# Paged attention with value rows of tokens c and c+16, and scores in run order

## Reference

```python
kc = k_cache[block_table].reshape(bsz, L, HK, D)
vc = v_cache[block_table].reshape(bsz, L, HK, D)
k_all = jnp.concatenate([kc, k], axis=1)
v_all = jnp.concatenate([vc, v], axis=1)
valid_c = jnp.arange(L)[None, :] < cache_seqlens[:, None]
valid = jnp.concatenate([valid_c, jnp.ones((bsz, seqlen), dtype=bool)], axis=1)
scores = jnp.einsum('bqhd,bkhd->bhqk', q, k_all) * SCALE   # k_all, v_all repeated 4 times over heads
scores = jnp.where(valid[:, None, None, :], scores, -1e+30)
probs = jax.nn.softmax(scores, axis=-1)
o = jnp.einsum('bhqk,bkhd->bqhd', probs, v_all)
```

## Time and profile before

| | |
|---|---|
| time, median of 3 runs | 1672.35 us (1672.19 to 1674.79) |
| profiled execution, its own time | 1670.93 us |
| its span, first to last instruction | 1669.1 us |
| mean granted TensorE clock | 0.996 |
| busy over the span: PE, PEld, DVE, ACT, POOL | 1611.0, 1407.2, 1113.8, 943.9, 303.9 us |
| `cached_attention`: first score product to last value product | 857.2 to 1455.6 us |
| moved by DMA over the span | 290.69 MB, mean 174 GB/s |

### The profile page before, as it was taken

One profiled execution on the slowest core, in us unless ns is written; L12 is line 12 of the kernel. 1 busy time (PEld: TensorE's weight loads), 2 busy tenths in 40 slices (PEclk: granted clock), 3 DMA queues, 4 the chain that ended last, 5 costly groups with the idle time before them and its releaser, 6 DMA issues. The chain is left out here.

```text
span 1669.1 us, 33975 instructions
## 1 busy us (share of the span) xinstructions
PE 1611.0 (97%) x10728; PEld 1407.2 (84%) x10728; DVE 1113.8 (67%) x2941; ACT 943.9 (57%) x2392; POOL 303.9 (18%) x306
## 2 busy tenths in 40 slices
PE   2899999999999999999979999999999999999998
PEld 2787888888888788888868999999999999977777
DVE  8404543454446657777767898898989889864443
ACT  3224223232322256667667999999999999822221
POOL 1000000000000146556531112111211211022210
PEclk9999999999999999999989999999999999999999
DMA  6621222201210333434567999999999999595401
GB/s 232 210 91 50 69 70 69 69 18 51 69 63 27 140 109 119 135 109 134 157 221 255 315 308 287 319 306 304 297 315 306 289 316 309 185 315 148 120 9 51
DMA packets 230095, 290.69 MB, mean 174 GB/s; under 512 B 17658, under 2 KB 181914, under 8 KB 221850
## 3 DMA queue, kind: packets, MB, share of 16 engines
q1 hardware_dynamic: 220826, 222.90, 42.5%
q0 software_dynamic: 9216, 67.11, 11.5%
HBM read 237.44 MB, written 50.41 MB: 172 GB/s over the span
## 5 line engine op out<-in xcount | busy, mean ns | idle before, releaser
L1602 PE MATMUL p_val<-probs_t,vals 128*128 128x128 f32 x2048 | 271.1, 276 | 1.7 <-DMA vals<-in_v_pages,rows_now 1.7
L1602 PEld LDWEIGHTS p_val<-probs_t,vals 128*128 128x128 f32 x2048 | 251.8, 193 | 2.0 <-DMA vals<-in_v_pages,rows_now 2.0
L1512 DVE CUSTOM_DVE_ANT_0 probs<-p_score,mask 128x544 f32<-128x544 f32 x256 | 184.4, 721 | 50.2 <-issue 40.6
L1417 ACT ACTIVATE probs<-probs,low 128x544 f32<-128x544 f32 x256 | 190.1, 743 | 0.7 <-DVE low L1512 0.7
L1581 PE MATMUL p_turn<-cst,probs 128*128 128x128 f32 x1024 | 166.3, 285 | 0.1
L1501 DVE TENSOR_TENSOR wo_lo<-keys,wo_hi 128x544 fp32r<-128x544 f32 x224 | 161.8, 722 | 0.7 <-ACT wo_hi L1412 0.7
L1425 ACT ACTIVATE probs_t<-p_turn 128x512 f32<-128x512 f32 x256 | 149.2, 583 | 19.9 <-PE p_turn L1581 19.7
L457 PE MATMUL p_tile<-w_hi,y_hi 128*128 128x512 f32 x384 | 156.7, 408 | 2.4 <-PEq L470 2.4
L1071 POOL TENSOR_TENSOR w_lo<-w_raw,w_hi 128x512 fp32r<-128x512 f32 x44 | 57.8, 1319 | 548.2 <-DVE w_hi L1109 531.1
L1412 ACT ACTIVATE wo_hi<-keys 128x544 fp32r<-128x544 f32 x224 | 145.7, 651 | 20.4 <-PE p_score L459 18.7
L457 PE MATMUL p_score<-wo_hi,q_hi 128*128 128x288 f32 x448 | 149.4, 333 | 1.8 <-DVE wo_lo L1501 0.8
(11 more groups left out here) (218 smaller groups left out, 3538.8 us busy)
## 6 DMA issues: line engine op xcount, KB each, us to landing
keys<-in_k_pages SPq DMA_DIRECT2D x512, 128.0 KB, 4.7
qk_new<-x_res SPq DMA_DIRECT2D x80, 256.0 KB, 2.2
x_res<-qk_new SPq DMA_DIRECT2D x32, 512.0 KB, 7.1
o_new<-x_res SPq DMA_DIRECT2D x32, 512.0 KB, 6.8
w_raw<-in_w_vkq_t SPq DMA_DIRECT2D x12, 1024.0 KB, 5.7
w_raw<-in_w_qkv_t SPq DMA_DIRECT2D x10, 1024.0 KB, 8.4
toep<-kpad SPq DMA_DIRECT2D x32, 256.0 KB, 4.5
w_raw<-in_w_dense_t SPq DMA_DIRECT2D x8, 1024.0 KB, 5.4
```

Source lines behind the costliest of these rows:

```text
L1417: nc.scalar.activation(probs[:, i % 8, :], probs[:, i % 8, :], ACT.Exp, bias=low[:, i % 4:i % 4 + 1], scale=-1.0, accum_out=total[:, i % 4 ...
L1512: v.tensor_tensor_reduce(out=probs[:, i % 8, :], in0=score_at(i % 2, slice(0, KEYS)), in1=mask[:, i // HK, :], scale=1.0, scalar=3e38, op0 ...
L1602: mm = pe.matmul(p_val[:, h, half * P:(half + 1) * P], vals[:, slot, c // RUN, c % RUN * HK * D + k * D:c % RUN * HK * D + (k + 1) * D], p ...
```

## The change

A value row now holds tokens c and c+16 of a page in place of 2c and 2c+1: the host permutes `v_pages`, the gathers stay as they are. Scores, mask and probabilities of a head stand in the order of the runs: 272 columns for run 0 (tokens 0 to 15 of each of the 17 pages), then 272 for run 1 (tokens 16 to 31). `k_hi` and `k_lo` are written in that order, so the split reads 34 pieces of 16 elements from `keys`, where it read 17 of 32. The parts of the score products are the two runs, 272 columns each, and the PSUM columns are 240 to 784 for an even head and 752 to 1296 for an odd one. The unsplit products of k = 0 stream 17 pieces of 16 columns. The transposes read four blocks of 128 neighbouring columns, at 0, 272, 128 and 400. The gathering of the new keys' probabilities reads two pieces of 16 a head. The key positions behind the mask are permuted alike. No instruction is added or removed.

```diff
@@ -34,6 +34,7 @@
 RUN = 2
 GATHERS = CACHE // (P * RUN)
 KEYS = CACHE + S
+RUN_KEYS = KEYS // RUN
 SCALE = float(D) ** -0.5
 THETA = 10000.0
 EPS = 1e-6
@@ -93,8 +94,9 @@
     c[:, C_INVF:C_INVF + D // 2] = np.float32(1.0) / np.float32(THETA) ** (np.arange(0, D, 2, dtype=np.float32) / np.float32(D))
     c[:, C_SPOS] = p % S
     c[:, C_CAUSAL:C_CAUSAL + S] = np.where(np.arange(S)[None, :] <= (p % S)[:, None], 0.0, -BIG)
-    c[:, C_KEYPOS:C_KEYPOS + CACHE] = np.arange(CACHE)
-    c[:, C_KEYPOS + CACHE:C_PART] = -BIG
+    key_pos = np.full((RUN, NPP + 1, PSIZE // RUN), -BIG, np.float32)
+    key_pos[:, :NPP] = np.arange(CACHE).reshape(NPP, RUN, PSIZE // RUN).transpose(1, 0, 2)
+    c[:, C_KEYPOS:C_PART] = key_pos.reshape(1, KEYS)
     c[:, C_PART] = p
     per_page = PSIZE // RUN
     c[:, C_RUNPAGE:C_RUNPAGE + NPP] = np.arange(NPP)[None, :] % (P // per_page) == (p // per_page)[:, None]
@@ -1308,12 +1310,13 @@
         qk, v_new, o_dram = io["qk_new"], io["v_new"], io["o_new"]
         LAST = B // 2 - 1
         QUADS = RB // NEW
-        LONG, SHORT = 9 * PSIZE, 8 * PSIZE
-
-        ENDS = (slice(0, LONG), slice(SHORT, KEYS))
-        MIDDLES = (slice(LONG, KEYS), slice(0, SHORT))
-        FROM = (E - LONG, E + KEYS - LONG)
+
+        ENDS = (slice(0, RUN_KEYS), slice(RUN_KEYS, KEYS))
+        MIDDLES = (slice(RUN_KEYS, KEYS), slice(0, RUN_KEYS))
+        FROM = (E - RUN_KEYS, 2 * E - RUN_KEYS)
         score_at = lambda n, part: p_score[:, FROM[n] + part.start:FROM[n] + part.stop]
+        in_runs = lambda a: a.rearrange("p (r n c) -> p r n c", r=RUN, c=PSIZE // RUN)
+        of_head = lambda a, k: a[:, :, k, :].rearrange("p n (r c) -> p r n c", r=RUN)
         half_heads = lambda a, slot, n: a[:, slot, n * HQ * S // 2:(n + 1) * HQ * S // 2]
 
         QUERY_AT = {1: slice(P, HQ * S // 2), HK // 2: slice(HQ * S // 2, HQ * S)}
@@ -1409,7 +1412,7 @@
                     act.wait_ge(scores_done, r - 1)
                 if k in QUERY_AT:
                     nc.scalar.activation(q_hi[:, slot, QUERY_AT[k]], queries[:, slot, QUERY_AT[k]], ACT.Copy).then_inc(q_hi_ready, 1)
-                nc.scalar.activation(k_hi[:, i % 2, :].rearrange("p (n s) -> p n s", s=S), keys[slot][:, :, k, :], ACT.Copy).then_inc(k_hi_ready, 1)
+                nc.scalar.activation(in_runs(k_hi[:, i % 2, :]), of_head(keys[slot], k), ACT.Copy).then_inc(k_hi_ready, 1)
 
             def exponent(m, i):
                 r = m * RB + i
@@ -1432,7 +1435,8 @@
                     act.wait_ge(probs_ready, m * RB + i + 1)
                     if not (isinstance(n, int) and n < 2):
                         act.wait_ge(new_turned, n - 1)
-                    nc.scalar.activation(probs_n[:, q % 2, :, :], probs[:, q % 2 * NEW:(q % 2 + 1) * NEW, CACHE:KEYS],
+                    new = probs[:, q % 2 * NEW:(q % 2 + 1) * NEW, :].rearrange("p h (r n) -> p h r n", r=RUN)[:, :, :, CACHE // RUN:RUN_KEYS]
+                    nc.scalar.activation(probs_n[:, q % 2, :, :].rearrange("p h (r c) -> p h r c", r=RUN), new,
                                          ACT.Copy).then_inc(new_gathered, 1)
 
             def take_turned_new(m, q):
@@ -1498,8 +1502,8 @@
                     v.tensor_tensor(q_lo[:, slot, QUERY_AT[k]], queries[:, slot, QUERY_AT[k]],
                                     q_hi[:, slot, QUERY_AT[k]].bitcast(F32), ALU.subtract).then_inc(q_lo_ready, 1)
                 v.wait_ge(k_hi_ready, splits_to(m, i))
-                v.tensor_tensor(k_lo[:, i % 2, :].rearrange("p (n s) -> p n s", s=S), keys[slot][:, :, k, :],
-                                k_hi[:, i % 2, :].rearrange("p (n s) -> p n s", s=S).bitcast(F32), ALU.subtract).then_inc(k_lo_ready, 1)
+                v.tensor_tensor(in_runs(k_lo[:, i % 2, :]), of_head(keys[slot], k),
+                                in_runs(k_hi[:, i % 2, :]).bitcast(F32), ALU.subtract).then_inc(k_lo_ready, 1)
 
             def mask_scores(m, i):
                 r = m * RB + i
@@ -1559,8 +1563,8 @@
 
                 def product(part):
                     if k == 0:
-                        return pe.matmul(score_at(i % 2, part), queries[:, slot, 0:P],
-                                         keys[slot][:, part.start // S:part.stop // S, 0, :], start=True, stop=True)
+                        at = slice(part.start // RUN_KEYS * PSIZE // RUN, part.stop // RUN_KEYS * PSIZE // RUN)
+                        return pe.matmul(score_at(i % 2, part), queries[:, slot, 0:P], keys[slot][:, :, 0, at], start=True, stop=True)
                     return three_pass(pe, score_at(i % 2, part), q_hi[:, slot, k * P:(k + 1) * P], q_lo[:, slot, k * P:(k + 1) * P],
                                       k_hi[:, i % 2, part], k_lo[:, i % 2, part], True, True)
 
@@ -1578,7 +1582,8 @@
                 if not (isinstance(r, int) and r < 1):
                     pe.wait_ge(turned_taken, r)
                 for n in range(4):
-                    mm = pe.transpose(p_turn[:, n, :], probs[:, i % 8, n // RUN * P * RUN + n % RUN:(n // RUN + 1) * P * RUN:RUN], ident)
+                    at = n % RUN * RUN_KEYS + n // RUN * P
+                    mm = pe.transpose(p_turn[:, n, :], probs[:, i % 8, at:at + P], ident)
                 mm.then_inc(turned, 1)
                 if i % NEW == NEW - 1:
 
@@ -1892,7 +1897,7 @@
         "q_norm": lay(inputs["L0_cond2_q_norm_w"]),
         "k_norm": lay(inputs["L0_cond2_k_norm_w"]),
         "k_pages": lay(np.asarray(inputs["L0_cond2_k_cache"]).transpose(0, 3, 2, 1).reshape(PAGES, D, HK * PSIZE)),
-        "v_pages": lay(np.asarray(inputs["L0_cond2_v_cache"]).reshape(PAGES, PSIZE, HK * D)),
+        "v_pages": lay(np.asarray(inputs["L0_cond2_v_cache"]).reshape(PAGES, RUN, PSIZE // RUN, HK * D).transpose(0, 2, 1, 3).reshape(PAGES, PSIZE, HK * D)),
         "w_o_t": lay(np.asarray(inputs["L0_cond2_Wo"]).T),
         "lora_a": lay(np.asarray(inputs["L0_ffn_lora_A"]).reshape(LORA_N * RANK, E)),
         "lora_b_t": lay(np.asarray(inputs["L0_ffn_lora_B"]).transpose(0, 2, 1).reshape(LORA_N * RANK, E)),
```

## The result

The changed kernel takes 1662.57 us (median of 4 runs, 1661.82 to 1663.88) against 1672.57 us for the kernel before beside it. The two medians lie 10.0 us apart; the ratio on record is 0.9942 with an interval of 0.993 to 0.9955, which is 9.7 us less (7.5 to 11.7), or 0.6%. The forecast was 1661.2, 11.1 us less.

The account below looks back on a forecast made before the run. PE was taken to set the pace of an attention batch; plain columns in the transposes save 0.37 us in each of 30 batches, 11.1 us off 1672.35, so 1661.2 us, with 1657 to 1668 as the 8-in-10 range.

Parts of the forecast that it names:

- What bounds the kernel: Attention batch of 18.26 us: PE always has work in flight and sets the pace by distances between product starts.
- The transposes: Line 1581, 32 a batch: plain columns bring them to line 1185's 0.109 us each, 0.37 us off a batch.
- Rival (1): Line 1581: the column step is not what makes the transposes slow; nothing moves, 1672 us; chance 0.11.
- The halves: Score products in two parts of 272 columns: taken as nothing, 0.01 us a head either way.
- the split copies: ACT's key copy (line 1412) and DVE's subtraction (line 1501) in runs of 16: taken as nothing.
- the raw products: Products of heads without a split, streaming runs of 16: taken as nothing, at worst 2.9 us in all.
- The closest meeting of PE with ACT: Transposes at 1110.41 may start after ACT's copy of the turned columns ends at 1110.04: 0.37 us to spare.
- Rival (2): Line 1412: ACT takes over the pace from 0.14 us more per split, at the far bound 1726 us; chance 0.06.
- The size: Whole kernel: 30 batches x 0.37 = 11.1 us off, bounds 8.4 to 11.7.
- The forecast of the profiled execution: Profiled run of the changed kernel: 1659.8 us, taken to lie 1.42 below the median as before.

Follow-up runs that it names:

- e1: Kernel before with only the four transposes reading 128 neighbouring columns each, all else as before: 1661.26 us, ratio 0.9942.
- e9: Changed kernel with the projection stage's transposes (line 1185) reading every second column: 1669.19 us.
- e7: Changed kernel with one extra one-column ACT copy behind the split copy of every second head, 4 a batch: 1663.0 us.
- e8: Changed kernel with one extra one-column ACT copy behind every split copy, 7 a batch: 1669.93 us.
- e6: Changed kernel with split heads' parts at 288 and 256 columns again and ACT's result copy cut in two halves: 1659.74 us, ratio 0.9923.
- e5: Changed kernel with ACT's copy of a batch's result cut in two, the first value products waiting for the first half only: 1660.95 us.
- e2: Kernel before with the attention's transposes reading every third column: 1668.15 us.
- e3: Kernel before with the attention's transposes reading every fourth column: 1673.39 us.

## Why the prediction was right

**What bounds the kernel** held: PE has work in flight in the whole batch, before and after, and the stage became 10.0 us shorter. A batch is the sum of the distances between PE's starts, so that the two agree proves nothing by itself; what bears the claim out is that no new wait took more of the gain than the 0.027 us told below.

**The transposes** came out as reckoned from line 1185: 0.109 us each, 0.37 us a batch. The 3.88 us a batch that I read from starts rounded to 0.01 us were 3.85 by the exact ones, within the 0.03 that I had allowed, so the lower side that I took was the right one. The row of a like operation read in plain columns gave the price; e1 shows that the step alone is the cause, e9 that the step makes line 1185 slow in its turn.

**Rival (1)** fell with e1. The page that spoke for it, "SBUF — State Buffer" of the Trainium skill, section "Door 1: The DMA port swizzle (why `[64,N]` ≈ `[32,N]`)", lets two accesses to a 16-byte line run at full rate and sets a penalty on one access a line. For these f32 weight loads the trace does not agree: 206 ns at step 2 against 141 in plain columns, and only 209 at step 4. The measurement decides.

**The halves, the split copies, the raw products** were each taken at nothing. ACT's 651 and DVE's 722 ns are unchanged, the raw products take 0.92 us as before (1102.05 to 1102.97), and the halves lie within the 0.01 us a head that I allowed. (The 0.23 us in their line is the distance behind a product of 512 columns in the earlier trace rows, 785.32 to 785.55.)

**The closest meeting of PE with ACT** is the step that failed. I gave 0.37 us, at the transposes at 1110.41. The result copy was closer, with 0.17 us by the starts and about 0.02 by what the products can do after it, and it turned into a wait of 0.027 us once a batch, 0.8 us in all. The sum had no term for it. I had looked at the waits that occur for every head and not at the one that occurs once a batch.

**Rival (2)** did not come: the key copies stayed at 651 ns. But its threshold was too high. I let ACT decide from 0.14 us more a split, by its idle time; e7 shows PE losing 0.08 us at 0.09 on every second split, and the place was the result copy. By e7 and e8, 0.10 us spread over the three splits that lie ahead of that copy is all that ACT can take up, so I estimate that some 0.03 us a split would begin to cost PE time.

**The size.** 30 x 0.37 = 11.1 was forecast; 30 x 0.31 = 9.3 came by the batch and 9.7 (7.5 to 11.7) by the time. Of the 0.06 us, 0.03 are the result copy and the rest, 0.02 to 0.05, lies in the score products. Its cause is open: the halves may be part of it (e6 is 0.02 us a batch shorter than e5), but e2 and e3 show 0.02 to 0.03 without them. The forecast of the profiled execution, 1659.8 us, missed: I took it to lie 1.42 us below the median again, and at 1663.88 it was the slowest of the four. Batch 1 still begins with a wait for keys, 3.74 us, as the earlier trace rows had it with 3.58:

```profile
883.74 1.73 PE L1567 MATMUL p_score<-keys,x_res 128*128 128x272 f32 x3 [3.74 <-DMA keys<-in_k_pages]
```

## What to carry to other kernels

Where products with 128 columns follow one another, the way their weights are read can set the distance, as here, where the step of the columns alone made 0.120 us of 0.109: look for the same operation on plain columns elsewhere in the trace before believing a layout is free, and move the permutation to where it costs nothing, here a host-side order and the split copies. When an engine that sets the pace gets faster, list for every wait in its order, also those once a batch, how much earlier its releaser ended, and compare that with the shortest such distance in a run in which the wait does bind; what lies between the two is the room. The idle time of the other engine is not: only the part of it that lies ahead of the releaser counts.

## What was not expected of the hardware

A weight load of 128 f32 columns costs nearly the same at steps 2, 3 and 4 (206, 199 and 209 ns against 141 in plain columns), and step 3 is the fastest of them: 18.14 us a batch against 18.26 and 18.32. An ACT instruction on one column has a record of 190 ns, but the next one starts 0.09 us after it began: most records of ACT in these batches run on for some 0.1 us past the start of the next.
